# Odd output tiles by Strassen's seven block products, and the residual through the weights, in a LoRA and state-space layer on one core

## The reference

```python
# x: (128, 64, 1024), every example b has its own adapter ids[b]
y  = einsum('bsd,od->bso', x, W) + bias                    # base product, W: (1024, 1024)
y += einsum('bsr,bor->bso', einsum('bsd,brd->bsr', x, A[ids]), B[ids])   # LoRA, rank 16
x1 = x + y
K  = 2 Re sum_n Ct[h,n] exp(dtA[h,n] * l)                  # 64 filters of 1024 taps
y2 = causal_convolution(x1, K) + x1 * D                    # along the last axis, per head h
out = x1 + y2 * (l < length[b])
```

## Time and profile before

| | us |
|---|---|
| three executions | 1139.37, 1139.67, 1144.08; median 1139.67 |
| the profiled execution's own time | 1139.35 |
| its span, from the first to the last instruction | 1137.7 |
| PE busy, first stage and second | 99% of the span |
| DVE busy | 719.8 (63%) |
| ACT busy | 530.2 (47%) |
| moved by DMA | 202.47 MB |

### The profile page before, as it was taken

How to read it: one execution, slowest core, us unless ns; L and a number is a source line. 1 busy time by engine, 2 the same in 40 slices (tenths; PEclk the granted TensorE clock), 3 DMA queues, 4 the chain that set the end, 5 groups by cost and what they waited for, 6 DMA issues and landing times.

```text
span 1137.7 us, 15785 instructions
## 1 busy us (share of the span) xinstructions
PE 1125.5 (99%) x5824; PEld 973.6 (86%) x5824; DVE 719.8 (63%) x1108; ACT 530.2 (47%) x888; POOL 30.5 (3%) x78
## 2 busy tenths in 40 slices
PE   7999999999999999999999999999999999999998
PEld 6888888888888888888888888888889999999997
DVE  5856465646556465646556465644268888888886
ACT  5333160433142160433151261422268888888885
POOL 1000000000000000000000000000000000000000
PEclk9999999999999999999999999999999999999999
DMA  7594525354252525344252525253649998989873
GB/s 228 152 62 162 193 67 190 141 127 169 72 184 63 186 75 185 118 147 165 71 189 71 185 75 185 102 149 119 215 167 320 313 314 307 315 303 322 297 284 130
DMA packets 125441, 202.47 MB, mean 178 GB/s; under 512 B 17267, under 2 KB 99124, under 8 KB 121396
## 3 DMA queue, kind: packets, MB, share of 16 engines
q1 hardware_dynamic: 125364, 201.46, 56.1%
HBM read 117.41 MB, written 84.02 MB: 177 GB/s over the span
## 4 chain that ended last, share of the span: by engine, by line
PE 94%; DMA 4%; SPq 1%; DVE 0%; issue 0%; ACT 0%; DVEq 0%
PE acc L1224 57%; PE acc L1276 24%; PE acc L1205 5%; PE acc L1236 5%; PE acc L1299 3%; DMA exponent_scratch<-k_vt 2%; DMA x_scratch<-x_sb 1%; DMA w_raw<-w_t 1%; PE acc L1246 0%; SPq L349 0%; SPq L358 0%; SPq L353 0%; DMA ids_sb<-ids 0%; DVE w_lo L753 0%; DVE x_sb L798 0%
## 5 line engine op out<-in xcount | busy, mean ns | idle before, releaser
L1224 PE MATMUL acc<-x_hi,w_hi 128*128 128x512 f32 x1024 | 401.2, 392 | 8.8 <-DVE x_lo L753 7.5
L1224 PE MATMUL acc<-x_hi,w_lo 128*128 128x512 f32 x1024 | 399.2, 390 | 0.0
L1224 PE MATMUL acc<-x_lo,w_hi 128*128 128x512 f32 x1024 | 399.2, 390 | 0.0
L1224 PEld LDWEIGHTS acc<-x_hi,w_hi 128*128 128x128 f32 x1024 | 192.5, 188 | 46.3 <-DVE w_lo L753 7.5
L1224 PEld LDWEIGHTS acc<-x_hi,w_lo 128*128 128x128 f32 x1024 | 192.5, 188 | 41.0
L1224 PEld LDWEIGHTS acc<-x_lo,w_hi 128*128 128x128 f32 x1024 | 192.6, 188 | 35.4
L798 DVE SCALAR_TENSOR_TENSOR x_sb<-acc,bias_sb,x_raw 128x512 f32<-128x512 f32 x128 | 94.3, 748 | 193.0 <-PE acc L1236 178.9
L596 ACT ACT_TABLE_LOAD x16 | 20.5, 1283 | 235.0 <-DVE eg_f L916 235.0
L1276 PE MATMUL acc<-u_hi,f_hi 128*128 128x512 f32 (+1 forms) x320 | 129.7, 405 | 0.0
L1276 PE MATMUL acc<-u_hi,f_lo 128*128 128x512 f32 (+1 forms) x320 | 119.6, 374 | 0.0
L1276 PE MATMUL acc<-u_lo,f_hi 128*128 128x512 f32 (+1 forms) x320 | 118.0, 369 | 0.0
(11 more groups left out here) (155 smaller groups left out, 1432.9 us busy)
## 6 DMA issues: line engine op xcount, KB each, us to landing
x_scratch<-x_sb SPq DMA_DIRECT2D x16, 2048.0 KB, 7.3
out<-out_sb SPq DMA_DIRECT2D x63, 512.0 KB, 5.5
x_raw<-x_t SPq DMA_DIRECT2D x15, 2048.0 KB, 12.3
u_raw<-x_scratch SPq DMA_DIRECT2D x14, 2048.0 KB, 13.0
wq_raw<-state_scratch SPq DMA_DIRECT2D x16, 1024.0 KB, 7.8
a_raw<-lora_a SPq DMA_DIRECT2D x128, 64.0 KB, 4.4
b_raw<-lora_b SPq DMA_DIRECT2D x128, 64.0 KB, 4.4
state_scratch<-g_sb SPq DMA_DIRECT2D x16, 512.0 KB, 3.1
```

The lines of the kernel that those rows point to most:

```text
L1224: mm = pe.matmul(acc[:, n % O_BANKS, :], w, m, start=k == 0 and i == 0, stop=False)
```

## The change

The tiles of the output are separated into even and odd ones. The four even tiles are computed as before, in two banks in place of four, and ACT takes them out (`even_out`). The odd ones are four tiles, with eight k blocks and 512 columns; W and x are each cut into 2 x 2 blocks (two tiles x four k blocks; four k blocks x half of the columns), and the 2 x 2 product is made of seven block products in the form of Winograd: four sums of weights (S1 to S4, made once in group 0), four sums of x (T1 to T4, made by DVE in each group), and seven products p1 to p7, each 2 tiles x 4 k blocks x 3 matmuls of 256 columns. Partial sums that two outputs share are carried by ACT from bank to bank (`seed_b`, `seed_c`, `seed_e`). The adapters' part is added to the odd tiles by `end_11`, `end_12`, `end_22` and `end_21`. The residual x is no longer added by `make_x1`: an identity is added to the diagonal blocks of W.

To make room: x_raw has one buffer, and x of group g+1 is loaded after T4 of group g; raw adapters lie over the two halves of x1_sb (b_raw over the even one, a_raw and h_own over the odd one), so they are loaded after the stores of those halves; the store of a group is made in an even and an odd half, in pieces of 512 bytes, laid out so that the second stage reads 8 KB and more at a time; g_sb and e_sb share a place. `filter_exponents` moves from group 0 to group 1, and the first unit of the filters to its end. In the second stage the columns are ordered by group, chunk and example in place of chunk and example, the banks are given out anew, and ACT's and DVE's first steps are reordered; the number and sizes of its matmuls stay. The diff, cut to its core:

```diff
-    x_raw = [place(f"x_raw{i}", [P, NT, N], F32) for i in range(2)]
-    x_split_at = cursor[0]
+    x_raw = place("x_raw", [P, NT, N], F32)
...
+    t_lo = place("t_lo", [P, 3, HALF, NH], F32R)
+    t_raw = place("t_raw", [P, 3, HALF, NH], F32, at=t_at)
+    t_hi_at = cursor[0]
...
+    x1_at = cursor[0]
+    x1_sb = place("x1_sb", [P, 2, heads, HALF, G], F32)
+    X1_BYTES = heads * HALF * G * 4
+    b_raw = place("b_raw", [P, NT, P], F32, at=x1_at)
+    h_own = place("h_own", [R2, N], F32, at=x1_at + X1_BYTES)
...
-    H_BANK = O_BANKS
-    K_BANK = O_BANKS + 2
-    V_BANK = 2
+    A_BANK, D_BANK, B_BANK, C_BANK, O_BANK, H_BANK, E_BANK = 0, 1, 2, 3, 4, 6, 7
+    O_BANKS = 2
+    K_BANK = D_BANK
...
+    def slot_of(g, place):
+
+        if g == 1:
+            return 0 if place == PER_GROUP - 1 else None
+        j = 1 + PER_GROUP * (g - 2) + place
+        return j if g >= 2 and j < ALL_UNITS else None
...
             def load_x(g):
-                sp.dma_start(x_raw[g % 2][:, :, :].rearrange("p t n -> p (t n)"), x_t[g]).then_inc(ld_x[g % 2], 16)
+                sp.wait_ge(c_t["T4"], g)
+                sp.dma_start(x_raw[:, :, :].rearrange("p t n -> p (t n)"), x_t[g]).then_inc(ld_x, 16)
...
+            def store_x1(g, par):
+                if par == 0:
+                    sp.wait_ge(c_even, HALF * (g + 1))
+                else:
+                    sp.wait_ge(c_21, g + 1)
+                    sp.wait_ge(c_12, g + 1)
+                    sp.wait_ge(c_22, g + 1)
+                sp.dma_start(x1_d[:, :, par, g, :].rearrange("q p w -> p q w"),
+                             x1_sb[:, par, :, :, :].rearrange("p (q h) t b -> p q (h t b)", h=HQ))\
+                  .then_inc(st_x1[par], 16)
 
...
             for g in range(n_groups):
-                if g + 1 < n_groups:
-                    load_adapters(g + 1)
-                if g == 0:
+                if g >= 1:
+                    store_x1(g - 1, 1)
+                    sp.wait_ge(st_x1[0], 16 * g)
+                    for i in range(G):
+                        load_b(i, adapter_of(g, i))
+                if g < LAST:
+                    sp.wait_ge(c_alo, 2 * (g + 1))
+                    if g > 0:
+                        sp.wait_ge(st_x1[1], 16 * g)
+                    for i in range(G):
+                        load_a(i, adapter_of(g + 1, i))
+                if g == 1:
                     store_exponents()
                     load_zb(0)
-                if 1 <= g <= FILTERS_DONE:
-                    filter_stores(g)
-                if g == FILTERS_DONE + 1:
+                filter_stores(g, 0)
+                if g < LAST:
+                    load_x(g + 1)
+                for c in range(n_chunks):
+                    if g == taps_group(c):
+                        store_k(c)
+                for place in range(1, PER_GROUP):
+                    filter_stores(g, place)
+                if g == FILTERS_DONE:
...
-                sp.wait_ge(c_x1, NT * (g + 1))
-                sp.dma_start(x1_d[g], x1_sb[:, :, :, :].rearrange("p h t b -> p (h t b)")).then_inc(st_x1, 16)
...
+            def biased(dst, src, tile):
+                return act.activation(dst, src, ACT.Identity, bias=bias_sb[:, tile:tile + 1])
+
...
+            def split_t(g, n):
+
+                act.wait_ge(c_t[n], g + 1)
+                if n == "T1":
+                    act.wait_ge(m_p6, g + 1)
+                elif n == "T4":
+                    act.wait_ge(m_p7, g + 1)
+                elif g > 0:
+                    act.wait_ge(m_p5 if n == "T2" else m_p4, g)
+                if g == 0 and n == "T2":
+                    act.wait_ge(st_pad, 16)
+                copy(t_hi[:, HI_SLOT[n], :, :], t_raw[:, LO_SLOT[n], :, :]).then_inc(c_thi[n], 1)
...
+            def seed_b(g):
+
+                act.wait_ge(m_p1, g + 1)
+                if g > 0:
+                    act.wait_ge(c_12, g)
+                copy(acc[:, B_BANK, :], acc[:, A_BANK, :]).then_inc(c_seed_b, 1)
+
+            def seed_c(g):
+                act.wait_ge(m_p6, g + 1)
+                if g > 0:
+                    act.wait_ge(c_22, g)
+                copy(acc[:, C_BANK, :], acc[:, B_BANK, :]).then_inc(c_seed_c, 1)
+
+            def seed_e(g):
+                act.wait_ge(m_p7, g + 1)
+                copy(acc[:, E_BANK, :], acc[:, C_BANK, :]).then_inc(c_seed_e, 1)
...
+            def even_out(g, i):
+
+                act.wait_ge(m_even, HALF * g + i + 1)
...
+                biased(x1_sb[:, 0, :, i, :].rearrange("p h (c b) -> p c h b", c=2),
+                       acc[:, o_bank(g, i), :].rearrange("p (c h b) -> p c h b", c=2, b=GH), 2 * i).then_inc(c_even, 1)
...
+                act.wait_ge(m_11, g + 1)
+                act.wait_ge(c_hlo, 2 * (g + 1))
+                act.wait_ge(c_alo, 2 * min(g + 2, n_groups))
...
             for g in range(n_groups):
-                if g == 0:
-                    filter_pre()
-                if 1 <= g <= FILTERS_DONE:
-                    filter_steps(g)
-                if g + 1 < n_groups:
-                    split_a(g + 1)
+                if g > 0:
+                    out_21(g - 1)
+                    seed_b(g)
+                    split_t(g, "T2")
+                    split_b(g)
+                    take_h(g)
+                    split_h(g)
+                    split_t(g, "T3")
+                    if g < LAST:
+                        split_a(g + 1)
+                    filter_step(g, 0)
+                    even_out(g, 0)
+                    seed_c(g)
+                    out_11(g)
+                    split_t(g, "T1")
+                    filter_step(g, 1)
+                    even_out(g, 1)
+                if g > 0:
+                    filter_step(g, 2)
+                if g < LAST:
                     for t in range(NT):
                         split_x(g + 1, t)
...
+            def weight_sums():
+                a11, a12, a22 = (v_raw[:, j, :, :, :] for j in (A11, A12, A22))
+                a21 = a21_raw[:, :, :, :]
+                corner_residual(A22, ld_v22, 2)
+                dve.wait_ge(ld_v21, 16)
+                v_sum(S1, a21, a22, ALU.add, 3)
+                v_sum(S3, a11, a21, ALU.subtract, 4)
+                v_sum(S2, v_raw[:, S1, :, :, :], a11, ALU.subtract, 5)
+                dve.wait_ge(ld_v12, 16)
+                v_sum(S4, a12, v_raw[:, S2, :, :, :], ALU.subtract, 6)
...
+
+            def t1(g):
+                if g > 0:
+                    dve.wait_ge(m_p5, g)
+                dve.tensor_tensor(t_slot("T1"), x_block(0, 1), x_block(0, 0), ALU.subtract).then_inc(c_t["T1"], 1)
+
+            def t3(g):
+                if g > 0:
+                    dve.wait_ge(m_p7, g)
+                dve.tensor_tensor(t_slot("T3"), x_block(1, 1), x_block(0, 1), ALU.subtract).then_inc(c_t["T3"], 1)
+
+            def t2(g):
+                if g > 0:
+                    dve.wait_ge(m_p4, g)
+                dve.wait_ge(c_t["T1"], g + 1)
+                dve.tensor_tensor(t_slot("T2"), x_block(1, 1), t_slot("T1"), ALU.subtract).then_inc(c_t["T2"], 1)
+
+            def t4(g):
+
+                dve.wait_ge(m_p6, g + 1)
+                link(dve.tensor_tensor(t_slot("T4"), x_block(1, 0), x_block(1, 1), ALU.subtract))
+                dve.tensor_tensor(t_slot("T4"), t_slot("T4"), t_slot("T1"), ALU.add).then_inc(c_t["T4"], 1)
...
+                if g > 0:
+                    out_22(g - 1)
+                    t1(g)
+                    t3(g)
+                    t2(g)
+                    split_t(g, "T2")
+                    split_b(g)
+                    keep_own(g)
+                    split_h(g)
+                    split_t(g, "T3")
+                    if g < LAST:
+                        split_a(g + 1)
+                    filter_step(g, 0)
+                    t4(g)
+                    taps(g)
+                    split_t(g, "T1")
+                    filter_step(g, 1)
+                if g > 0:
+                    filter_step(g, 2)
                 if g < LAST:
-                    split_a(g + 1)
                     for t in range(NT):
                         split_x(g + 1, t)
...
+                split_t(g, "T4")
+                out_12(g)
+                if g == FILTERS_DONE:
+                    finish_unit(*divmod(ALL_UNITS - 1, UNITS))
...
+            def even_base(g, i):
+                n = HALF * g + i
                 if n >= O_BANKS:
-                    pe.wait_ge(c_x1, n - O_BANKS + 1)
-                if g == 0 and t > 0:
-                    pe.wait_ge(c_wlo, t)
+                    pe.wait_ge(c_even, n - O_BANKS + 1)
...
+            def product_hi(g, j, bank, hi, opens):
+
+                if g == 0:
+                    pe.wait_ge(c_vlo, v_order.index(j) + 1)
+                for i in range(QT):
+                    for k in range(HALF):
+                        for s, w in enumerate((v_hi, v_lo)):
+                            pe.matmul(bank_part(bank, i), w[:, j, k, i, :], hi[:, k, :],
```

(127 more changed lines are left out.)

995 lines of the change are left out of this document (549 added, 446 removed).

## The result

The changed kernel takes **1342.98 us** (median of 4 executions, 1340.07 to 1346.92) against 1139.62 for the kernel before on the same chip: a ratio of 1.1776, with a 95% interval of [1.1732, 1.182]. The profiled execution took 1341.29. Forecast: 1338, range 1270 to 1400.

What follows compares the result with a forecast made beforehand. TensorE, 99% busy, bounds the kernel, so new waits cost time. Span 1137.7 + 146 (13 groups) + 47 (groups 0, 1) + 0 (group 15) + 2 (second stage) + 3 (clock) = 1335.7, plus 1.65 outside: 1338 us, range 1270 to 1400.

Steps and rivals of the forecast that it cites:

- steps 3 and 4: ACT's queue: split_a and filter_step 0 precede even_out 0, which even_base 2 needs; ACT's functions (4.5 or 4.1 us) follow DVE's unit.
- step 6: Group's tail: both queues split next x (8 x 0.63 us on ACT), after filter_step 2, ahead of seed_e and T4 that p4 needs.
- step 1: Group start: b loads wait for the even store (6 us), then 8 x 1.12 us on SP; b lands at 15, a at 24.5.
- Step 5: DVE: t4 (2.4 us) stands behind filter_step 0; only then can SP issue the next x load, taking 8.2 to 15.3 us.
- kind C: Groups 4, 9, 14: even_out 1 at 44.4 (ready 35.1), x split to 56.9, p4 at 59.2; group ends at 62.9 us.
- A: Groups 2, 7, 12: no ACT work in filter place 0; p4 at 55.8, TensorE ready at 47.5; group ends at 59.5 us.
- D: Groups 5, 10: even_out 0 at 35.5, no further stall; group ends at 60.4 us.
- Kinds B and E: B (groups 3, 8, 13): functions in places 0 and 1, 64.3 us; E (6, 11): even outputs late, p4 at 64.4, 68.1 us.
- Short stalls: Rival, 12%: adapter loads land 3 to 5 us earlier, DVE and ACT overlap better; groups 55 to 57, total 1180 to 1275 us.
- Worse than the walk: Rival, 11%: adapter loads take 4.4 us, the store over 10, clock loss of 1.4 us shows everywhere; total 1420 us.
- Gain kept: Rival, 5%: ACT reaches even_out 0, even_out 1 and seed_e before TensorE; the 34 us saving stays, total 1105 us.
- Products not cheaper: Rival, 2%: 256-column matmuls with new weights take over 0.13 us each, so nothing is saved.

Runs made afterwards that it cites:

- Experiment 1: Changed kernel with ACT's even outputs, seed_c, out_11 and split of T1 ahead of its filter steps: 1296.08 us, ratio 1.1369.
- Experiment 5: Changed kernel with ACT's outputs ahead of its filter functions, the third filter step behind the group's tail, and the even store before that step's pieces: 1265.03 us.
- Experiment 2: Changed kernel with SP reading each adapter id once and keeping it in a register from a load to b load: 1281.08 us, ratio 1.1238.
- 7: Changed kernel with the edits of experiments 2, 3 and 5 together, plus SP's b loads ahead of the odd store: 1186.18 us, ratio 1.0403.
- experiment 8: Kernel 7 with T4's sum, the taps and the split of T1 ahead of the first filter step on DVE: 1234.03 us, ratio 1.0822.
- best version: Kernel 7 with the split of the next group's a rows later in ACT's and DVE's queues (experiment 11): 1153.91 us, ratio 1.0129.
- experiment 3: Changed kernel with the exponents' store behind the load of x(2) on SP, load_zb(0) behind group 2's a loads: 1326.98 us, ratio 1.1641.
- experiment 11: Kernel 7 with the next group's a split moved behind the first filter step on ACT and the split of T1 on DVE: 1153.91 us.

## Why the prediction was right, and what was off

**The reading** (PE has no room, so new waits are paid in time; three in-order queues become one chain) held. Experiment 1 shows steps 3 and 4 of the walk as causes: moving ACT's steps alone gives 47 us back. Experiment 5 shows step 6: with the third filter step behind the tail on ACT and DVE, and the even store ahead of its pieces, it is 78. Experiment 2 shows step 1: SP's second reading of the ids cost 62. Step 5 was tried only on top of 7 (experiment 8), where T4's sum ahead of the filter step cost 48. The helpers' work was sized well: DVE is busy for 36.9 us a group and ACT for 27.6, forecast 37 and 29.

**The walk against group 4** (kind C; forecast, then measured, from p1 at 290.0): b landed 15, 14.7; even output 0 may be taken from 25.7, 24.5; even output 1 done 44.4, 43.6; x split to 56.9, 55.7; end 62.9, 61.8. Group lengths, from the starts of adapters_down (167.99 for group 2, 982.04 for group 15):

| kind | groups | forecast | measured |
|---|---|---|---|
| A | 2, 7, 12 | 59.5 | 64.2, 63.7, 64.5 |
| B | 3, 8, 13 | 64.3 | 60.8, 61.4, 62.2 |
| C | 4, 9, 14 | 62.9 | 61.8, 62.6, 62.1 |
| D | 5, 10 | 60.4 | 60.0, 60.7 |
| E | 6, 11 | 68.1 | 65.2, 64.9 |

The sum is 814 for 817, partly by errors that cancel. Kind A was 4.6 short: it makes two g units in a row from one buffer, and the second waits for the store of the first (DVE g_tmp, 14.7 us, once in each of groups 2, 7 and 12; the last row of the waits). The walk had left that wait out. Kinds B and E were 3 too long.

**The same sum by what PE did** shows more cancelling. Forecast for 13 groups: 13 x 48.9 = 636 of work and 181 idle, with +3 of clock beside them. Measured: 130 idle (814.0 - 684.35). The same work takes 652 at full clock, by the undisturbed groups above, so about 32 of the 684 come with the lower clock (0.92 on the mean; an estimate). Idle time was put 51 too high, and two terms too low:
- *The work and the saving.* An undisturbed group was put at 48.9 and the saving at 2.1. Measured are 49.7 without the filter taps and 50.4 with them, which the forecast had left out; like for like the saving is 1.4 (51.10 - 49.68, 51.89 - 50.45). Adapters_down takes 3.84 for 32 matmuls where it took 3.75, 0.120 apart for 0.117, and the products have the same pitch (16 in 1.92). On the 168 + 64 matmuls of this size that is 0.65 us, nearly all of the missing 0.7. Over groups 3 to 14 of the best version (50.5 on average) 1.1 are left of the saving.
- *The clock* was put at +3, since I let nearly all of it hide in the next wait. One stall of 8.92 us cost 6.92 - 5.24 = 1.7, near the 1.4 of the earlier trace rows, but there are 14 waits at L1490 and 4 at L1521. As time in which PE was busy it is about 32 us; how much of it a later wait would have hidden was not separated. The Trainium skill ("TensorE: Matmul & The Clock Gate", HAM oscillation) warns of this pattern; the trace agrees, with one dip of the clock after another through the first stage.

**Group 1** (86 forecast; 85.2 between the starts of adapters_down) held. **Groups 0 and 1** together were put at +47 and cost +51.2; the missing 4 are group 0's: its product 1 began at 39.5 where I had 37.8, the load of x(1) went out at 60.0 in place of 55, and group 1 began at 79.9 in place of 75. The mechanism of group 1 is in the chain of waits of the kernel after:

```profile
116.07 26.08 DMA exponent_scratch<-k_vt
...
142.60 10.71 DMA x_raw<-x_t
```

The store of small pieces takes 26.1 us, as the earlier trace rows had it, and the load of x stands behind it in SP's queue; experiment 3 took 20 us out of that group.

**Group 15** was put at 0 and cost 5.6: PE waits 5.3 for the low half of h. It has neither filter steps nor an a split, so I took it as undisturbed; but its b rows still wait for the store of the even half. **Second stage**: +2 forecast, +1.7 measured.

**The store** of a half, in runs of 512 bytes, landed in 5.2 us at the median (below), where I took 6 between 3.7 and 7.3.

```profile
DMA to landing us min/median/max: 5.0/5.2/11.6
```

The Trainium skill ("DMA: Bandwidth & Descriptors", Specifications) has such runs at line rate, which would give 3.7; half of the bytes took 71% of the time. So the measurement does not bear out 3.7, whether by the short runs or because a smaller transfer takes more than its share of the time; no run tells the two apart.

**Rivals.** Short stalls: refuted, the groups take 60 to 65 us, not 55 to 57. Worse than the walk: refuted, adapter loads landed in 1.8 (a) and 2.0 (b) at the median, the store in 5.2. Gain kept: refuted for this order of queues; experiment 11 has its groups from 3 on at 49.7 to 51.3, under the 51.6 at which it was to decide, and the whole is still slower, by what lies outside them. Products not cheaper: refuted, 0.120 a matmul, well under 0.13.

## What to carry to other kernels

A saving on the bounding engine is worth what its helpers' queues let through: before counting it, write down for each in-order queue which instruction the bounding engine needs next and what stands ahead of it. When one wait is removed, look where the next comes up: six edits took back 189 of 203 us, and one of them (b loads first) cost 6 us until the late a split took away what it had pushed back. Sharing one buffer between a store's source and the next load's target (b_raw in x1_sb) ties a group's start to the store's landing, and then register reads between the loads lengthen the group: here 4 us of them were worth 3.9 us a group.

## What the runs showed that was not expected

- The same 32 matmuls of 256 columns came 0.117 apart before and 0.120 after (3.75 and 3.84 us), without a wait and at full clock. Why stays open.
- A copy of 512 columns from PSUM to PSUM on ACT takes 0.58 us, less than the 0.63 of 512 columns from SBUF to SBUF.
- Replacing Exp and Sin by Copy, which also ends the change of function tables, saved 33 us where their own time suggested 60: in these steps ACT waits for DVE (170.4 us in all) more than it computes.
